# Value products directly behind the scores, both heads' transposes in a row, and new orders for four queues

## The reference, cut to what matters

```
x = layernorm(x + attention16(x))                 # 16 heads of 64, softmax over 256 keys ("first attention")
x = layernorm(x + routed_ffn(x))                  # small chains on VectorE
x = layernorm(x + linear_and_window_attention(x)) # window of 65 keys
h = layernorm(x)                                  # second attention: q and k normalised, causal,
o = causal_attention16(h) @ Wo                    # 16 heads of 64 over halves of 128 tokens
x = layernorm(x + moe(layernorm(o)))              # 8 experts, 128 -> 512 -> 128, all of them, gated
# softmax: probs = exp(s - max) / sum ; out = probs @ v
```

## Time and profile before

| what | value |
|---|---|
| median of the two executions shown | 2324.43 us (2324.02 to 2324.85) |
| the profiled execution, its own time | 2327.11 us |
| its span, first to last instruction | 2325.3 us |
| PE busy | 2189.3 us, 94% |
| DVE busy | 1605.0 us, 69% |
| ACT busy | 1352.6 us, 58% |
| POOL busy | 849.2 us, 37% |
| chain that ended last | PE 81%, DVE 9%, ACT 5%, POOL 3% |

### The profile page before, as it was taken

One profiled execution on the slowest core, in us unless ns is written; L12 is line 12 of the kernel. 1 busy time (PEld: TensorE's weight loads), 2 busy tenths in 40 slices (PEclk: granted clock), 3 DMA queues, 4 the chain that ended last, 5 costly groups with the idle time before them and its releaser, 6 DMA issues.

```text
span 2325.3 us, 44711 instructions
## 1 busy us (share of the span) xinstructions
PE 2189.3 (94%) x16091; PEld 1523.0 (65%) x16091; DVE 1605.0 (69%) x5015; ACT 1352.6 (58%) x3784; POOL 849.2 (37%) x1010
## 2 busy tenths in 40 slices
PE   8989999999999999999999999999999999999897
PEld 5656666856668566676667665676666756667465
DVE  5666686686766866678765878658686686766752
ACT  5336574765647755476555767466564764646452
POOL 3314561054510654107521256114561054510630
PEclk9999999999999999999999999999999999999999
DMA  4000001010010100110001100001001010010001
GB/s 153 28 1 1 1 2 46 11 33 1 1 55 2 33 1 1 55 33 1 1 10 46 33 1 1 28 28 33 1 1 46 10 33 1 2 42 6 33 1 50
DMA packets 24726, 50.48 MB, mean 22 GB/s; under 512 B 3316, under 2 KB 3900, under 8 KB 24252
## 3 DMA queue, kind: packets, MB, share of 16 engines
q1 hardware_dynamic: 24508, 47.63, 6.3%
HBM read 45.52 MB, written 2.10 MB: 20 GB/s over the span
## 4 chain that ended last, share of the span: by engine, by line
PE 81%; DVE 9%; ACT 5%; POOL 3%; issue 1%; DMA 0%; SPq 0%; DVEq 0%; ACTq 0%
PE ps L1488 10%; PE ps L1509 10%; PE ps L601 5%; PE ps L667 5%; PE ps L650 4%; PE ps L1521 4%; PE ps L867 4%; PE ps L1422 4%; PE ps L1439 4%; PE ps L905 4%; PE ps L1394 3%; PE ps L798 3%; PE ps L781 3%; PE ps L834 3%; PE ps L1383 2%; PE ps L605 2%
## 5 line engine op out<-in xcount | busy, mean ns | idle before, releaser
L1047 POOL TENSOR_TENSOR rstd<-ve,half_neg 128x4 f32<-128x4 f32 (+1 forms) x56 | 66.8, 1193 | 972.4 <-DVE ve L1028 972.4
L1509 PEld LDWEIGHTS ps<-wbuf,QK 128*128 128x128 f32 x2048 | 265.4, 191 | 108.2 <-issue 103.3
L1304 POOL TENSOR_TENSOR E<-E,ri 128x512 f32<-128x512 f32 x240 | 249.4, 1041 | 149.7 <-DVE ri L1102 148.8
L1612 ACT ACTIVATE QK<-ps,cols 128x512 f32<-128x512 f32 x256 | 173.9, 687 | 219.3 <-PE ps L1488 218.9
L1738 POOL TENSOR_TENSOR work<-work,ri 128x128 f32<-128x128 f32 x480 | 231.6, 506 | 108.7 <-DVE ri L1661 107.0
L1488 PE MATMUL ps<-h2T,wbuf 128*128 128x512 f32 x512 | 270.9, 617 | 0.1
L1509 PE MATMUL ps<-wbuf,QK 128*128 128x128 f32 x2048 | 269.0, 275 | 0.0
L928 ACT ACTIVATE E<-ps,nm 128x256 f32<-128x256 f32 x480 | 224.5, 479 | 57.9 <-DVE nm L1095 56.9
L1731 POOL TENSOR_TENSOR rn<-ss,half_neg 128x8 f32<-128x8 f32 x120 | 196.0, 1638 | 156.5 <-DVE ss L1637 154.0
L1572 ACT ACTIVATE work<-ps,nm 128x128 f32<-128x128 f32 x480 | 200.2, 433 | 66.9 <-DVE nm L1653 66.0
L1653 DVE CUSTOM_DVE_ANT_0 ps<-ps,causal 128x128 f32<-128x128 f32 (+1 forms) x512 | 167.5, 389 | 31.0 <-PE ps L1422 30.1
(11 more groups left out here) (280 smaller groups left out, 4558.6 us busy)
## 6 DMA issues: line engine op xcount, KB each, us to landing
wbuf<-in_w SPq DMA_DIRECT2D x128, 256.0 KB, 3.2
xT<-in_xT SPq DMA_DIRECT2D x8, 256.0 KB, 3.5
xr<-in_xr SPq DMA_DIRECT2D x8, 256.0 KB, 3.8
bias_t<-in_bias_t SPq DMA_DIRECT2D x1, 2048.0 KB
out_y<-xn SPq DMA_DIRECT2D x8, 256.0 KB, 2.1
wqkv<-in_wqkv SPq DMA_DIRECT2D x1, 1536.0 KB
wo<-in_wo SPq DMA_DIRECT2D x2, 512.0 KB, 7.8
rows<-in_rows SPq DMA_DIRECT2D x1, 531.0 KB, 6.6
```

The source lines that it names most:

```text
L1304: nc.gpsimd.tensor_tensor(L.E[:, g % 4, :, :], L.E[:, g % 4, :, :], L.ri[:, g, :].unsqueeze(2).broadcast_to((P, NT, S)), ALU.mult)\
L1509: last = nc.tensor.matmul(bank2[2 + x % 2][:, t * P:(t + 1) * P], hid[:, x % 2, c, t * P:(t + 1) * P], w2[:, x % WB, c, :], start=(c == 0) ...
```

## The change

Two things. In both attentions the value products of an iteration move one step forward, so that they stand directly behind the scores, and the transposes of heads 2u-2 and 2u-1 then follow each other in the generator with nothing of their own attention between them. And the table `ORDER` is replaced: all thirteen of its strings are new, each of the same length with the same count of each digit. No instruction is added or taken away on any engine. The waits that each step has are the same. The one string of SyncE puts the load of the next pair behind the weights of the sixth expert instead of the fifth.

```diff
@@ first_heads_pe @@
                     last.then_inc(sem_of(L, "sc"), 1)
                 yield
-                if 1 <= u <= HP:
-                    weights0_T(pe, L, n, 2 * u - 2)
-                yield
                 if u >= 2:
                     v = u - 2
                     for i in range(2):
...
                     last.then_inc(sem_of(L, "av"), 1)
+                yield
+                if 1 <= u <= HP:
+                    weights0_T(pe, L, n, 2 * u - 2)
                 yield
                 if 1 <= u <= HP:
                     weights0_T(pe, L, n, 2 * u - 1)
@@ second_heads_pe: the same, with weights_T @@
...
@@ ORDER, two of its thirteen strings @@
     ("both", "tensor"):
-        "010011111011011100101101011101110101110110101110010101010100111101010110101101010110010101110001"
-        "101011111011101011111011011101101110110110101110100101100010111101001010110101010011001010110101"
-        "001101001010110101010101010100111001100101111111111111101111111110111100110110110011000000000000"
-        "0000010000000100000000202000020000202200222222",
+        "001011110111101010110101101101111001101011010101011110010011100100111001111010110011010110011110"
+        "100011101011011101111111101010110111011011101101101111000110001101001011010100110101001101010011"
+        "100100111001001100111001101001001110110001111111111111011111111101111101110101100011000000000000"
+        "0000000011000200000000002000020000202202022222",
...
     ("both", "sync"):
-        "1111101111",
+        "1111110111",
```

More of the change, by code:

```diff
@@ L61 @@
     ("both", "vector"):
[L62 to L66, removed]
+        "001001101101110101111101111000101011111011111011010100111111011111100010101011100010010111000101"
@@ L67 @@
+        "010110010111101011101000001111101000000110111010110111111101101111111111101111101111111111111110"
+        "110111110111101011000011011010001101010100001011101001000110110010110100100010101101001010011010"
+        "001110001110000001010100000011111011101010111000000000000000000010000010000000010000000010000001"
+        "100000000010001010100010000000000111000110010101011110101110100010000000",
     ("last", "vector"):
-        "000000010000001011101001011101010100110111101010101111111111101100001111101001011010100010010101"
@@ L69 @@
-        "101001000111010001011011000101101100100110110010011011001001110100010111001001010100101010000000"
+        "000000100010111001011010110011010010111111011011110011000010111010111001011000100000111011010101"
+        "111000001111010001011101001001101100001110110010011101000101110100001110100101100100110010000000"
         "00000000000000000000000000000000000",
     ("first", "tensor"):
-        "101010000000101100100001111010011110000111000101100101100101101101011010101101100110001101100001"
@@ L73 @@
[L73 removed]
+        "001001010100010001101011010010010001011111000101110000111100010111000101110011110101110110001100"
+        "11010011012000020000200000000000000000000000000000000000000000000202202022222",
     ("both", "tensor"):
[L75 to L76 removed]
@@ L84 @@
-        "00000000000000000000000000000002220222222222",
+        "000101010100001100010110100111010001110001010110100110110001111110100101110001100100000010000000"
+        "00000000000000000000000000000020222022222222",
     ("both", "scalar"):
-        "110110001111010101011110111001111100100011111100011110000111101110100101110000101101101111111011"
-        "101011111111101111011110101100111010111010010110100110110001101010010110100011101001101001010110"
-        "011010100111011111111011111111111110111010111010101010000000000000000000000000000000022202022222"
+        "110101011011110010111010110101101110110101110010011100010110100101110111100100101100111110111111"
@@ L89 @@
+        "011011111011111110111011110101110011101100001110100110101001011010001110010110100101110001010011"
+        "110100101010111111101111111111111101111010111110101000000000000000000000000000000000022200222222"
         "222",
     ("last", "scalar"):
-        "000000001001110101010011011011100111011101011001111000001011100101101010011100000111100101101100"
-        "00111001011010110010000000000000001000000000000000000000000",
+        "000001000111001011100011101111100010001011110001111010001110100101101000101110010111100001111000"
@@ L93 @@
+        "00111001001110100101000000000000000000000000000100000000000",
     ("first", "gpsimd"):
-        "000001011100010101011101100110101000000000",
+        "000010011001010101101010101101110000000000",
     ("both", "gpsimd"):
-        "000110110111100001010111010110101010111111111111100110101001101010101001100101011010000010010",
+        "000111010110110001011010100101110110111111111111100101100101011010100101010101011001000011000",
     ("last", "gpsimd"):
-        "000101101101110011010100101010101100101101010100000",
+        "001011011010101011001010101011001101100101001100000",
@@ L1442, in second_heads_pe @@
                     last.then_inc(sem_of(L, "av"), 1)
+                yield
+                if 1 <= u <= HP:
+                    weights_T(pe, L, n, 2 * u - 2)
                 yield
```

12 lines of the change are left out of this document (4 added, 8 removed).

## The result

| | before | after |
|---|---|---|
| median of the executions shown | 2324.43 us (2) | 2400.41 us (2400.17 to 2400.65, 2) |
| profiled execution, own time (span) | 2327.11 (2325.3) | 2400.17 (2398.4) |
| ratio | 1 | 1.0311, interval 1.0278 to 1.0344 |

The account below looks back on a forecast made before the run. TensorE was taken to bound the full turn, with idle time only at the passes' starts. +7.2 (shapes) + 21.8 (pairs) - 15.7 (waits gone) = +13.3 on the median 2324.43 gave 2338 us, range 2308 to 2352.

Parts of the forecast that it names:

- part one: TensorE in all parts: added changes of shape between steps, about 0.15 us each, uncovered in the full turn; +7.2 us together.
- part two: Attention transposes with too little between them: the second waits for ScalarE's copy of the first; +21.8 us together.
- part three: First pass of each middle part: waits at its start and at 511.80 and 521.51 go, 2.24 us a part, -15.7 us.
- part four: Everything else: new orders of DVE, ACT and POOL covered by PE, SP's later loads without a waiter; nothing.
- first and last part together: The two end parts: shape changes 0.35 and 0.55 us, pairs two at 0.5 and 0.80 + 0.35; no waits go.
- B: Starts of the passes: part two's pairs cost nothing and the -15.7 holds; 2316 us, 2293 at most gain; chance 0.27.
- C: Full turn: value products wait for DVE's later copy, 0.1 to 0.3 us a turn; 2346 to 2361 us; chance 0.18.

Follow-up runs that it names:

- extra_change: Kernel before with four 128*128 transposes of the first attention moved one step earlier in each middle part's second pass, 28 more shape changes: 2339.6 us, ratio 1.0033.
- strings_alone: Kernel before with all thirteen new ORDER strings but the old step order, value products between the two transposes: 2412.4 us, ratio 1.0368.
- after_fill: Changed kernel with the old order transpose, value products, transpose in the second attention's last iterations: 2402.7 us, ratio 1.0322.
- fill_early: Changed kernel with the old step order in the second attention's last iterations and ScalarE's copy there one step earlier, ahead of the exponentials: 2398.4 us, ratio 1.0284.
- light_after: Changed kernel with VectorE's sum of squares reading 16 of 64 numbers per head: 2384.7 us, ratio 1.0243.
- swap_alone: Kernel before with only the new step order, value products ahead of both transposes in both attentions, and all old strings: 2467.9 us, ratio 1.0592.
- before_warm: Kernel before with spare matmuls added ahead of four waits of TensorE in the middle parts: 2322.7 us, ratio 0.9963.
- after_warm: Changed kernel with the six spare matmuls back behind L700 and L702 and spare matmuls added ahead of four TensorE waits in middle parts: 2377.8 us, ratio 1.0224.

## Why the prediction was wrong, step by step

Terms of the sum against the trace, us over the run, from starts of rows (accounted in detail on one middle part and taken seven times; the line between parts two and three is good to some 2 us):

| step of the forecast | forecast | measured |
|---|---|---|
| part one, changes of shape, middle parts | +6.3 | +6.4 |
| part two, pairs, middle parts: waits on ScalarE's copies | +19.6 | +25.6 |
| part three, waits that go: the other waits up to the end of the first pass | -15.7 | +6.0 |
| part four: second pass without these, first passes at half clock | 0 | +2.8 |
| part four: from the passes to L700, and the last sections | 0 | +27.0 |
| first and last part together | +3.1 | +5.5 |
| sum | +13.3 | +73.3 (73.1 between the profiles) |

**Part one was right.** 146 changes of shape a part instead of 140 at 0.15 us, a turn of 5.72 us for the 5.71 forecast, and the remainder in extra_change agrees. The Trainium skill, "TensorEngine Tiling (Array Packing)", Key Properties, says that changing the tiling mode drains TensorE. The trace agrees that a change costs time, 0.15 us.

**Part two was right in place and nearly in size, and wrong in mechanism where it counts.** Heads 8 and 9 lose 0.91, 12 and 13 lose 0.80, the forecast had 0.80 each; with the smaller ones, and the refill behind each wait, 3.7 us a part instead of 2.8. The forecast took the pair as the cause, so that "before, each of these pairs had at least value products of 0.8 between" seemed the whole protection. strings_alone has no bare pair and the same idle time there, and after_fill and fill_early showed a second bound of the same length behind the first. That the size came out near is in part luck. Who "repairs" the pair gets nothing.

**Part three failed, and it is the step that turned the sum's balance.** I took 2.24 us of waits as gone because the rows would have other neighbours. Those waits did go. But I asked only what would stand at the old waits, and not what the value products had been covering where they stood before. They had stood between the last transpose of k and the scores; two transposes earlier they cover neither of the last two copies of k. Those copies now stand between steps of TensorE with one short transpose beside them, which is the pattern of part two with VectorE's copy in ScalarE's place: 0.93 before L1406 and 0.44 before L1422. With them came 0.37 before the value products themselves, and by starts of rows 0.32 before L650 and 0.24 before L905. Instead of -2.24 a part it is +0.86, an error of 21.7 us over the run. VectorE's 92% in that stretch, which I used as a cap on the gain (1.8 us), is not what made the two larger waits: light_after took VectorE to 81% and they stayed. How much of the 0.93 comes of VectorE's new string, which puts both maxima ahead of the last product and its copy, and how much of TensorE's new order, no run separates.

**Part four failed, and it cost the most.** I wrote "nothing" for the strings of DVE, ACT and POOL and never followed the digits of the TensorE string beyond the attentions, where the spare matmuls changed place. I also held the stretch of the experts unchanged; its own sign ("moves by over 1 us a part") came true with 3.5. Of its 24.4 us, some 15 are the half clock behind idles of 0.7 to 0.9 us, as the two warm kernels show. The earlier trace rows shows a granted clock of 1.00 because its stretches end before that place; 27.3 us at half clock stood there in the kernel before already, and I had not looked.

**The rivals.** B, the starts win, did not occur, and neither did C in the full turn: from 599.5 to 631.5 us PE is busy 32.00 of 32.00. C's sign, value products that wait for VectorE's copy, is there at the start of the first pass (0.37 a part), where C had not looked. The slow side came from places that none of the rivals named. The chance for slower by over 2% was 0.04, too small by far: rival C was priced as one mechanism in the full turn, while new orders on four engines could lose in every stretch that is not full.

What stays open: no run has the new string of one engine beside the old strings of the others, so how the loss in the passes divides among the strings is not known. swap_alone and strings_alone show only that the old strings with the new step order, and the new strings with the old one, are both worse than the whole. The order of SyncE's loads was not tested by itself either. Whether some string for the new step order would beat the old kernel was not tried.

## What to carry to other kernels

A step that is moved to fill a wait stops covering what it covered before: look at the copies that ended under it in its old place, and price the new waits there, before the old wait is booked as a gain. A high busy share beside a wait does not say what makes it; make that engine lighter and see whether the wait goes (here one of 3.9 us went, and the two largest waits stayed). Before opening a pair of dependent steps, measure from the start of the round trip (scores) to the second step in both orders: if the distance stays equal when work stands between them, the pair is not the only bound. And when an order is searched anew, follow every moved filler to its new place: in this kernel idles of 0.7 to 0.9 us in a row cost twice, once as idle time and once through the clock of what came behind.

## What the runs showed of the hardware

Three idles of TensorE of 0.69, 0.77 and 0.87 us within 7 us, with small matmuls between, were followed by 6.8 us at a granted clock of 0.5 in the changed kernel. In the kernel before there are idles of 0.70, 0.69, 0.87 and 0.77 us in the same place, with the six spare matmuls between the second and the third, and they gave 3.4 us in some parts and none in others of one execution. Spare matmuls of 0.8 us ahead of the waits made that section run at full clock in five of seven parts of before_warm and six of after_warm; with them the kernel before gained 0.4%. What sets the fall in the last middle part, 10.2 us that stayed in both warm kernels, was not found.
